# The first two groups of sorted tokens are loaded in unit 14, in front of the first tiles' weights

## The reference

```python
xn = _layernorm(x)
# attention
q = (xn @ Wq.T); kv_latent = xn @ Wkv_down.T
k = kv_latent @ Wk_up.T; v = kv_latent @ Wv_up.T
attn = softmax(q k / sqrt(32)); a = (attn @ v) @ Wo.T
# experts: each token goes to one of the eight
keys = einsum('btd,d->bt', xn, wr) + br
expert_idx = mod(floor(keys).astype(int32), 8)
h = relu(xn @ W1[e] + b1[e]);  y = h @ W2[e] + b2[e]     # for e = expert_idx
out = x + a + y
```

## Time and profile before

| | |
|---|---|
| median of 3 runs | 500.4 us (497.17 to 500.55) |
| the profiled execution | 504.24 us, of which its span is 502.4 us |
| TensorE busy | 459.3 us, 91% of the span |
| VectorE | 414.3 us, 82% |
| GpSimd | 377.1 us, 75% |
| ScalarE | 345.9 us, 69% |
| DMA | 86.74 MB, 173 GB/s on average |

### The profile page before, as it was taken

How to read it: one execution, slowest core, us unless ns; L and a number is a source line. 1 busy time by engine, 2 the same in 40 slices (tenths; PEclk the granted TensorE clock), 3 DMA queues, 4 the chain that set the end, 5 groups by cost and what they waited for, 6 DMA issues and landing times.

```text
span 502.4 us, 15095 instructions
## 1 busy us (share of the span) xinstructions
PE 459.3 (91%) x4992; PEld 321.4 (64%) x4992; DVE 414.3 (82%) x883; ACT 345.9 (69%) x861; POOL 377.1 (75%) x399
## 2 busy tenths in 40 slices
PE   1877879999999999988999999997999999999995
PEld 1556445665656556557999999984666657656654
DVE  5988986787898898867888887885798898998884
ACT  3676466786777787757777777756687587777673
POOL 5755387887888878826777777767798888988972
PEclk9965799999999999989999999999999999999999
DMA  7994923454763798695887888835375556856522
GB/s 218 341 220 121 272 70 96 102 138 99 191 176 108 203 237 256 178 266 180 253 259 252 274 246 266 254 106 106 92 147 130 136 122 142 153 110 132 110 81 64
DMA packets 82826, 86.74 MB, mean 173 GB/s; under 512 B 10608, under 2 KB 66384, under 8 KB 82768
## 3 DMA queue, kind: packets, MB, share of 16 engines
q1 hardware_dynamic: 78672, 77.60, 57.5%
q0 software_dynamic: 4096, 8.40, 6.8%
HBM read 38.61 MB, written 22.04 MB: 121 GB/s over the span
## 4 chain that ended last, share of the span: by engine, by line
PE 42%; DVE 16%; issue 15%; POOL 13%; DMA 6%; SPq 4%; ACT 3%; POOLq 1%; ACTq 0%; DVEq 0%
POOL padd L591 12%; PE psum L1288 9%; PE psum L1253 8%; PE psum L1272 8%; DVE negm L992 6%; PE psum L1303 4%; PE psum L1330 4%; DMA stk<-mT 3%; SPq L325 3%; PE psum L1201 3%; PE psum L1202 2%; PE psum L1203 2%; DMA acc<-x 2%; DVE split L916 2%; DVE padd L877 1%
## 5 line engine op out<-in xcount | busy, mean ns | idle before, releaser
L726 ACT ACTIVATE prob<-psum 128x512 f32<-128x512 f32 x256 | 149.9, 593 | 94.9 <-PE psum L1272 67.4
L992 DVE TENSOR_REDUCE negm<-psum 128x2 f16<-128x512 f32 x256 | 170.7, 682 | 43.8 <-PE psum L1253 36.8
L644 POOL TENSOR_TENSOR padd<-prob 128x512 f32<-128x512 f32 x104 | 126.7, 1219 | 36.0 <-ACT prob L726 28.9
L1253 PE MATMUL psum<-stk 96*128 96x256 f16 x512 | 102.3, 282 | 9.9 <-DVE negm L992 7.1
L591 POOL TENSOR_TENSOR padd<-xTl,padd 128x512 f16<-128x512 f32 x71 | 82.3, 1159 | 36.4 <-DVE padd L1102 36.4
L1272 PE MATMUL psum<-stk 97*128 97x256 f16 x512 | 97.8, 275 | 6.2 <-DMA stk<-mT 3.5
L796 ACT ACTIVATE xTl<-psum,xn_all 128x128 f32<-128x128 f32 x284 | 81.1, 369 | 28.4 <-POOL padd L591 20.5
L609 POOL DMA_INDIRECT xsort<-xn_all,pos x64 | 66.9, 1046 | 14.0 <-issue 13.2
L624 POOL DMA_INDIRECT xn_all<-ysort,pos x64 | 66.0, 1032 | 14.6 <-issue 7.4
L1253 PEld LDWEIGHTS psum<-stk 96*128 96x128 f16 x512 | 41.7, 99 | 53.2 <-DVE negm L992 24.0
L1288 PE MATMUL psum<-prob,vt 128*32 128x256 f32 x1024 | 70.3, 393 | 0.9 <-ACT prob L726 0.7
(11 more groups left out here) (166 smaller groups left out, 886.2 us busy)
## 6 DMA issues: line engine op xcount, KB each, us to landing
stk<-split SPq DMA_DIRECT2D x192, 128.0 KB
xn_all<-wsplit SPq DMA_DIRECT2D x71, 258.0 KB, 4.2
xsort<-oT SPq DMA_DIRECT2D x9, 512.0 KB, 4.8
xTh<-xsort SPq DMA_DIRECT2D x18, 256.0 KB, 3.9
ysort<-xTh SPq DMA_DIRECT2D x18, 256.0 KB, 3.5
out<-acc SPq DMA_DIRECT2D x15, 256.0 KB
acc<-x SPq DMA_DIRECT2D x3, 1024.0 KB, 8.6
xn_all<-W SPq DMA_DIRECT2D x12, 256.0 KB
```

Source lines behind the costliest of these rows:

```text
L644: nc.gpsimd.tensor_tensor(padd[:, bb, hs], prob[:, bb, hs, 0, :], prob[:, bb, hs, 1, :], ALU.add).then_inc(pool_add, 1)
L726: nc.scalar.activation(prob[:, bb, h, :, :].rearrange("p a c -> p (a c)"), bank[st_bank(u, n)], ACT.Exp, scale=SCALE).then_inc(act_exp, 1)
L992: V.tensor_reduce(negm[:, k % 2, col:col + 2], bank[n % 2].rearrange("p (a c) -> p a c", a=2), AX.X, ALU.max, negate=True).then_inc(dve_ma ...
L1253: ins = mm(bank[n % 2][:, qc * T:(qc + 1) * T], stk[0:96, s, 1, h, t0 + qc * P:t0 + (qc + 1) * P], stk[0:96, s, 0, h, t0:t0 + T], start=Tr ...
```

## The change

The two waits for all scatters and the two `load_group` calls leave the head of unit 15, where they stood behind `first_weights()` and ahead of `load_stack(18)`. They now stand in unit 14, between `load_w2(5)` and `first_weights()`.

```diff
--- before.py
+++ after.py
@@ -365,6 +365,10 @@
                     load_w2(first)
                     load_w2(first + 1)
                 if u == 14:
+                    for par in range(2):
+                        sp.wait_ge(pool_scat[par], 128 * 4)
+                    load_group(0)
+                    load_group(1)
                     first_weights()
                 if u == 15:
                     load_w2(E - 2)
@@ -377,11 +381,6 @@
                     stores = half == 1 and not (first and k < 2)
                     if stores:
                         chunk, row = (s * 4, s * SB) if isinstance(s, int) else (sp.snap(s * 4), sp.snap(s * SB))
-                    if half == 0 and u == NU // 2 - 1:
-                        for par in range(2):
-                            sp.wait_ge(pool_scat[par], 128 * 4)
-                        load_group(0)
-                        load_group(1)
                     if not (last and k >= 1):
                         load_stack(u + 3, k + 3)
                     if not (last and k == 3):
```

## The result

The changed kernel took 504.91 us (median of 14 runs, 498.81 to 506.94) beside 500.68 us for the kernel before (14 runs). The ratio on record is 1.0053, interval 1.0028 to 1.0077; it leaves out the one slow run of the 14 (506.94 us). So the change costs about 2.6 us, as the means of the remaining runs also say (501.1 and 503.7 us); the two medians alone are 4.2 us apart. The forecast was +1.4 us and 501.8 us. By the ratio, the 500.4 us from which the forecast started become 503.1 us, which lies in the range of 497.9 to 503.4 us; the upper end of the interval (504.3 us) and the plain median do not.

A forecast was written before the change was run, and what follows sets the result against it. A ring of GpSimd, VectorE and ScalarE sets the pace, started by TensorE's token stall. The 3.4 us head start is lost waiting for `w2`, and half clock makes +1.4 us: 500.4 becomes 501.8 us, range 497.9 to 503.4.

The forecast's parts named there:

- step 4: At `output(0)`: TensorE idles 3.3 us for the last `load_w2`, the head start goes, half clock follows; +1.4 us in sum.
- Step 1: Token groups on SP's queue: issued at 214.1 us, landed before TensorE wants them, so the 1.94 us stall goes in full.
- rival (d): Token loads issued too late to help, weights still late: +1.4 to +2, at most 502.4 us; chance 0.05.
- Step 2: Start of the experts: without the token stall, at full clock, ScalarE's first relu gets a head start of 3.4 us.
- Step 3: Weights behind the moved loads on SP: first ones issued at 217.7 us, 4.5 us later; last `load_w2` lands at 230.9.
- the landing of the last `load_w2`: Transfer TensorE needs before `output(0)`: expected at 230.9 us, bounds 229.4 to 232, leaving TensorE idle 3.3 us.
- The clock term: Half clock behind TensorE's idle stretch at `output(0)`: tile 4 1.0 us late instead of 0.2 early, tile 5 another 0.4.
- Rival (a): Same TensorE wait for `w2`, but the clock stays full: -0.2 to 0, 500.3 us; chance 0.2.
- Rival (b): `w2` lands early, part of the head start lives: gain 1.6 us, 498.8 us; chance 0.15, the whole 0.07.
- The full head start: `w2` doesn't hold TensorE at all, so the whole 3.4 us are won: 497.0 us; chance 0.07.
- Rival (c): New idle stretch of TensorE starts a long low clock in the expert phase; 16 us of it gives 510 us; chance 0.03.

The follow-up runs named there:

- e2: Changed kernel with the register load for the eight experts moved ahead of the scatter waits; ratio 1.0006 to the kernel before.
- e4: Changed kernel with 44 extra matmuls keeping TensorE at work ahead of its wait for `load_w2`; ratio 0.9994 to the kernel before.
- e3: Changed kernel with the last two `load_w2` ahead of the stack and the row of maxima in unit 15; ratio 0.9994 to the kernel before.
- e1: Changed kernel with the last two `load_w2` right behind the two group loads, ahead of the first weights; ratio 0.9892 to the kernel before.
- e8: Changed kernel with registers loaded ahead of the scatter waits and the last two `load_w2` ahead of the stack; ratio 0.9908 to the kernel before.
- e6: Changed kernel with registers loaded ahead of the scatter waits and the last two `load_w2` right behind the groups; ratio 0.9918 to the kernel before.
- e7: Kernel before with only the two scatter waits moved to unit 14, group loads left in unit 15; ratio 1.0092 to the kernel before.
- e5: Kernel before with 16 extra matmuls ahead of the first token transpose, to fill TensorE's wait; ratio 0.9961 to the kernel before.

## Why the prediction was right, and where a size was off

The result, by the ratio, lies in the range, on the side that was forecast, and the mechanism is the one of step 4.

Step 1 held: no wait for `xsort`, groups issued within 4.5 us of `load_w2`, and with it rival (d) falls. Step 2 held to a tenth: a head start of 3.5 us for the 3.4 forecast. Step 3, the first weights: forecast 3.05 us ahead of the end of the sums (217.7 and 220.75), measured 3.1 us ahead (216.38 and 219.46). Two small slips in step 2 changed nothing: 225.41 to 226.90 is 1.49 us and not 1.45, and 222.6 + 0.8 is 223.4, which makes the forecast head start 3.5 us.

The term that was mis-sized is the landing of the last `load_w2`. Forecast was a start of `output(0)` 10.2 us after the sums and an idle stretch of 3.3 us; measured were 12.5 and 5.6. From the first weight load to the end of the wait were 15.6 us (216.38 to 231.96). SP took 1.98 us for the pair where it took 1.00 before, but that is the smaller part: e2 and e4, where it took 0.99 us, have 15.1 (212.93 to 228.05) and 15.2 (216.86 to 232.02), so it goes with some 0.4 us. The rest, 1.9 us, is the transfers. The prediction took 1.8 us off its 14.8 us for the two groups that no longer stand between the weights and w2, and e2 and e4 show that nothing came off for them. e3 shows the other lever: without the stack in front it was 12.3 us (217.69 to 229.99).

The clock term was right in kind and size for tile 4: 1.25 us (3.09 against 1.84 us from `output(0)` to ScalarE), forecast 1.2. The low stretch was longer than the ones before it in the rows: it began within the wait and not behind it, and lasted to about 236 us. e4 puts the whole at 2.1 us, where the prediction had 1.6. Rival (a), the wait at full clock, is e4 and is what did not happen. Rival (b) is e2 and e3: part of the head start lives when w2 lands earlier, and they come out level with the kernel before. The gain of 1.6 us in (b) left out the half clock, which by the prediction's own rows follows an idle stretch of 1.9 us; e2 and e3 had it, behind waits of 3.2 and 2.6 us. The full head start, "if `w2` doesn't hold TensorE at all", is e1, and it gave more than the 3.4 us (4.0 in the phase). Rival (c), a lasting low clock, did not occur.

The sum in the profile of the phase is +3.6 us; the timed runs say +2.6. The parts ahead of and behind the phase, which the change doesn't touch, were 1.3 and 1.1 us shorter in the profile after, and single executions differ by as much. Counted from the last row maximum, `output(0)` starts 2.2 us later than before, and from it to the last `hidden_low` are 1.4 us more (106.7 against 105.4); together the 3.6 us. The forecast had `output(0)` level with the kernel before. With the landing at its measured size the prediction's sum would have been +3.7 us, 504.1 us, which is above its range: that the timed runs came out inside it owes something to luck.

The Trainium skill's floor of about 600 ns for a `tensor_load` ("DMA: Bandwidth & Descriptors", "Latency and other measured facts") is not the price that this queue paid. With the load between them groups and weights were 3.4 us apart, and 1.4 us in e2 without it, so the load and what it holds up cost 2.0 us.

## What to carry to other kernels

When a load is moved forward in an in-order DMA queue together with the wait that guards it, price the wait by everything behind it, down to the last consumer: here the weights, the stack and the row of maxima had cover, and the last `load_w2` behind them all, for which TensorE waits once, did not. The cure was to bring that one forward too, ahead of transfers that could be late (e1), or to shorten what stands in front of it (e8). And an idle stretch of TensorE is paid twice if the clock falls behind it; a filler of matmuls during a wait shows how much that is.

## What the runs showed that I had not expected

The same idle stretch does not always bring half clock. TensorE waits about 2.2 us for the row of maxima of unit 17 in e1, e6 and e8. The timelines of TensorE, e1 first:

```profile
344.72 0.39 PE L1270 MATMUL psum<-stk 97*128 97x256 f16 x2 [2.23 <-DMA stk<-mT]
```

```profile
344.47 0.39 PE L1270 MATMUL psum<-stk 97*128 97x256 f16 x2 [2.21 <-DMA stk<-mT]
```

And the stretch behind it, e1 first, then e6:

```profile
345.00:350.00 5.00, 5.00 (x41) 2.32 (x39) 2.33 (x4) 3.24 (x7) 2.92 (x3) 0.66 0.43 109
```

```profile
345.00:350.00 5.00, 5.00 (x55) 3.41 (x54) 4.15 (x8) 4.70 (x12) 3.62 (x4) 1.00 0.53 121
```

The clock falls in e1 and not in e6, nor in e8, and in that place the three kernels don't differ. e7 has 2.21 us of idle there too and stays at 1.00. In the table "behind" is 164.4 to 166.0 us for the profiles with a low stretch near 350 us (before, after, e1, e2, e3, e5) and 161.6 to 163.2 us for those without (e4, e6, e7, e8), so it seems worth some 2 us of a run and may be one source of the spread of the times. The timed runs point the same way: of the 48 runs of the kernel before that were taken beside the experiments, the 12 with a mean granted clock of 0.974 or more took 499.4 us on average, and the 29 with 0.968 or less took 502.2 us. None of this was tried by itself, and in e4 the idle stretch there was also shorter (1.56 us).
